# Routing to the experts: from phases of its own into the second attention stage

## The chip, the core and the metric

The program runs on one core of one Trainium2 chip (trn2). The metric is the device time of one execution in microseconds: the median of three runs. TensorE (PE) multiplies matrices and transposes, VectorE (DVE) and ScalarE (ACT) work element by element, GpSimd (POOL) works element by element and issues indirect DMAs, SyncE (SP) issues all other DMAs. Each engine runs its own instructions in the order in which they are written; between engines only semaphores order them.

## The reference

Two layers. Each adds a cross attention of `x` (32 x 112 x 256) over a context (32 x 375 x 256, 16 heads of 16), gated by a tanh, and then a gated feed-forward part. The first layer's is three matrices of plus and minus one (256, 1024, 1024, 256) with ReLU between. The second layer's is a mixture of 8 experts: each of the 3584 rows goes to the expert with the largest logit, and each expert takes the first 448 rows that choose it:

```python
    probs = jax.nn.softmax(xf.astype(jnp.float32) @ Wr, axis=-1)
    eidx = jnp.argmax(probs, axis=-1)
    p_tok = jnp.take_along_axis(probs, eidx[:, None], axis=1)[:, 0]
    onehot = jax.nn.one_hot(eidx, E, dtype=jnp.int32)
    rank_all = jnp.cumsum(onehot, axis=0) - onehot
    rank = jnp.take_along_axis(rank_all, eidx[:, None], axis=1)[:, 0]
    keep = rank < cap
    ...
    xe = xf[dispatch]
    h = jnp.maximum(jnp.einsum('ecd,edf->ecf', xe, W1), 0.0)
    ye = jnp.einsum('ecf,efd->ecd', h, W2)
```

`xf` is the layer-normalised output of the second attention; `ye`, times the row's probability and a gate, is added to the row it came from. The rank of a row among those of its expert depends on all rows before it.

## The kernel before

The program is a sequence of phases, each a block in which every engine has its own list of instructions; at the end of a phase all engines meet and SP clears the phase's semaphores one by one (L93 to L97): setup, queries 0, attention 0, FFN, queries 1, attention 1, then `moe_phases`: logits, ranks, experts.

**Attention** (`attention_phase`, used for both layers) is unrolled over 32 batch rows. In step `s` five rows are in work at once, `p`, `g`, `x`, `d`, `e` being the rows 1 to 5 steps back: `p`'s keys are made (`make_keys`, with a low half `k_low` from VectorE, L1053, on which the second half of the keys and the values wait), `x`'s values are made and its row maxima reduced (`rows`, 16 of them, through a ring of three PSUM banks), `d`'s scores go in 12 units through TensorE (`score_unit`), ScalarE's exponential (`weigh_up`, L947) and POOL's mask (`mask_unit`, L697; POOL masks 8 of the 12), and are multiplied with the values at the end of the step (`weigh`); `e`'s heads are turned, normalised, turned back, projected (L851) and added to `x_sum` (`add_output`, L1046), which SP stores. The order within a step is written out by hand in each engine's `body`. The head bank (bank 6) and the work bank (bank 7) each serve several of these in turn.

**The FFN** takes groups of four batch rows, eight groups. A group goes through 16 tiles `z`: 8 of the first inner layer (4 matmuls each) and 8 of the second (16 each), four PSUM banks in turn; each tile is split by ScalarE and VectorE (`low_hidden`, L1214) into a high and a low half. Between them the next group `s` is normalised: statistics behind tile 4 (`normalise`, L1185), scaling behind tile 6 (`normalise_end`, L1199), transposes behind tile 11 (`turn`), their low half behind tile 12, the mask's transposes behind tile 13. VectorE also makes the next attention's masks behind tiles 8 to 10 (L1227 to L1239).

**The logits phase** loads the second attention's output again in groups of four, normalises it, turns it (L1450) and multiplies it with the router's matrix in fp32 (L1441). **The ranks phase** finds for all 32 rows at once the largest logit, the probability, and the rank: one product with a triangle of ones counts within a batch row, one with all ones makes the rows' totals, and a scan of VectorE additions makes the running sums. **The experts phase** begins with 32 indirect DMAs of POOL, one per batch row, which write the normalised rows, their weight and their number to `expert_in` (L1706). SP issues the weights of expert 0, waits for all scatters, and loads the rows (L1671 to L1678). ScalarE and VectorE split the weights (L1765, L1805) and rows (L1790, L1830) into high and low halves; L1738 and L1752 are the experts' two layers, L1696 the gather of the old rows and L1701 the scatter of the results.

## Time and profile before

| | us |
|---|---|
| median of 3 runs (1806.5 to 1809.34) | 1806.68 |
| the profiled execution | 1801.03 |
| its span, first to last instruction | 1799.0 |
| TensorE busy | 1509.3 (84%) |
| VectorE, ScalarE, POOL busy | 1081.4, 800.7, 848.6 |

The span in 40 slices of 45 us, busy share in tenths:

```profile
PE   1739999999997799999957379999999995509996
DVE  4727777777774455555437267777777763515663
ACT  3316666666664222222213146666666652114441
POOL 1347777777775000000013447777777761064332
PEclk9959999999998899999988589999999996559999
```

Slices 4 to 13 are the first attention, 14 to 21 the FFN, 24 to 33 the second attention, 34 to 36 logits, ranks and scatter, the last four the experts. Times of instructions below are from this one profiled execution. A row of a timeline with `x8` stands for eight instructions in succession; the time is from the first's start to the last's end. Matmuls are pipelined: two starts 0.19 us apart, not the 0.35 us of each, say how long one holds the engine.

### The profile page before, as it was taken

The page shows a single profiled execution, that of the slowest core. Times are in us where ns is not written, and L with a number is a line of the kernel's source. Part 1 is how long each engine was busy: PE and PEld are TensorE (multiplying, and loading weights), DVE is VectorE, ACT ScalarE, POOL GpSimd, SP SyncE. Part 2 cuts the span into 40 slices and gives each one's busy share as a digit, 9 for nine tenths or more (in the row PEclk, how much of TensorE's full clock was granted, in tenths as well). Part 3 has the DMA queues.
Part 4 walks back from the last instruction along what each step waited for, and adds up shares of the span by engine and source line. Part 5 has one row for each costly group of instructions (what it writes and reads, how often), then busy time and mean ns, then how long its engine had stood idle before and what let it go on. Part 6 is the DMA issues. An engine that isn't in the chain of part 4 may idle for free. (4 is left out here: it accounts for less than half of the span.)

```text
span 1799.0 us, 40766 instructions
## 1 busy us (share of the span) xinstructions
PE 1509.3 (84%) x15271; PEld 1089.3 (61%) x15271; DVE 1081.4 (60%) x3493; ACT 800.7 (45%) x1822; POOL 848.6 (47%) x794
## 2 busy tenths in 40 slices
PE   1739999999997799999957379999999995509996
PEld 0317777777775356655633157777777774507775
DVE  4727777777774455555437267777777763515663
ACT  3316666666664222222213146666666652114441
POOL 1347777777775000000013447777777761064332
PEclk9959999999998899999988589999999996559999
DMA  7654454444430212222127545665565622035440
GB/s 230 220 105 96 95 111 105 97 104 107 100 80 20 59 59 64 69 91 60 33 76 224 95 106 122 126 117 116 113 128 116 110 45 69 26 120 171 134 149 17
DMA packets 225378, 183.62 MB, mean 102 GB/s; under 512 B 70314, under 2 KB 218735, under 8 KB 225192
## 3 DMA queue, kind: packets, MB, share of 16 engines
q1 hardware_dynamic: 219560, 171.36, 40.1%
q0 software_dynamic: 5632, 9.78, 1.7%
q8 instruction: 117, 1.92, 0.5%
q14 instruction: 69, 0.57, 0.1%
HBM read 99.53 MB, written 48.49 MB: 82 GB/s over the span
## 5 line engine op out<-in xcount | busy, mean ns | idle before, releaser
L947 ACT ACTIVATE probs_a<-bank 125x448 f32<-125x448 f32 x768 | 387.9, 541 | 27.4 <-PE bank L807 11.3
L697 POOL TENSOR_TENSOR probs_a<-probs_a,keep_a 125x448 int32<-125x448 int32 x256 | 285.0, 1135 | 122.1 <-ACT probs_a L947 121.9
L697 POOL TENSOR_TENSOR probs_a<-probs_a,mask_keep 125x448 int32<-125x448 int32 x256 | 285.1, 1135 | 105.6 <-ACT probs_a L947 105.4
L1021 DVE CUSTOM_DVE_ANT_0 masked_scores_a<-bank,mask_add_a 112x375 bf16<-112x375 f32 x512 | 259.4, 546 | 111.1 <-PE bank L778 107.2
L1021 DVE CUSTOM_DVE_ANT_0 masked_scores_a<-bank,mask_add 112x375 bf16<-112x375 f32 x512 | 259.3, 546 | 92.2 <-PE bank L778 88.6
L778 PE MATMUL bank<-k_stack_a,q_stack_a 96*128 96x375 f16 x1024 | 292.5, 327 | 9.6 <-issue 3.0
L807 PE MATMUL bank<-q_stack_a,k_stack_a 97*128 97x224 f16 x1536 | 252.4, 259 | 11.2 <-DMA q_stack_a<-max_t_a 10.3
L1335 PE MATMUL bank<-h0h_f,ffn_w 128*128 128x448 f16 x512 | 180.7, 353 | 10.8 <-DVE h0l_f L1214 10.8
L807 PEld LDWEIGHTS bank<-q_stack_a,k_stack_a 97*128 97x128 f16 x1536 | 145.8, 98 | 71.3 <-DMA q_stack_a<-max_t_a 11.8
L1335 PE MATMUL bank<-h0l_f,ffn_w 128*128 128x448 f16 x512 | 180.5, 353 | 0.0
L1174 POOL DMA_DIRECT2D x_after_ffn<-y_f x8 | 5.9, 741 | 344.7 <-DVE y_f L1221 344.7
L823 PE MATMUL bank<-probs_a,values_a 125*32 125x112 f32 x6144 | 161.7, 260 | 2.9 <-POOL probs_a L697 2.9
L823 PEld LDWEIGHTS bank<-probs_a,values_a 125*32 125x32 f32 x6144 | 144.8, 110 | 23.9 <-issue 19.6
L705 POOL TENSOR_TENSOR ctx_low_a<-ctx_in_a,ctx_high_a 128x375 f16<-128x375 f32 x128 | 112.9, 903 | 69.6 <-ACT ctx_high_a L925 69.6
L778 PEld LDWEIGHTS bank<-k_stack_a,q_stack_a 96*128 96x128 f16 x1024 | 99.6, 98 | 53.5 <-DVE row_max_a L1021 11.2
L747 PE MATMUL bank<-ctx_high_a,wk_high 128*128 128x375 f16 x256 | 87.2, 340 | 53.3 <-POOL ctx_low_a L705 48.5
L970 ACT ACTIVATE heads_t_a<-bank 128x448 f32<-128x448 f32 x64 | 34.8, 543 | 217.3 <-PE bank L823 217.3
L1286 ACT ACTIVATE h1h_f<-bank 128x448 f16<-128x448 f32 x64 | 34.8, 543 | 167.1 <-PE bank L1335 167.1
L1214 DVE SCALAR_TENSOR_TENSOR h1l_f<-bank,h1h_f 128x448 f16<-128x448 f32 x64 | 40.0, 624 | 111.1 <-ACT h1h_f L1286 111.1
L768 PE MATMUL bank<-wv_high,ctx_high_a 128*128 128x256 f16 x384 | 104.9, 273 | 1.6 <-DVE k_low_a L1053 1.5
L768 PE MATMUL bank<-wv_high,ctx_low_a 128*128 128x256 f16 x384 | 104.6, 272 | 0.0
L768 PE MATMUL bank<-wv_low,ctx_high_a 128*128 128x256 f16 x384 | 104.5, 272 | 0.0
(201 smaller groups left out, 3121.5 us busy)
## 6 DMA issues: line engine op xcount, KB each, us to landing
k_stack_a<-k_high_a SPq DMA_DIRECT2D x256, 96.0 KB, 4.1
ctx_in_a<-in_ctx_dram SPq DMA_DIRECT2D x64, 375.0 KB, 3.4
w_in_e<-in_L_ffn_W_dram SPq DMA_DIRECT2D x16, 1024.0 KB, 8.4
k_stack_a<-k_low_a SPq DMA_DIRECT2D x128, 96.0 KB, 4.3
q_stack_a<-q_split SPq DMA_DIRECT2D x128, 84.0 KB, 3.3
x_and_bias<-xb_q SPq DMA_DIRECT2D x16, 448.0 KB, 4.4
q_split<-high_q SPq DMA_DIRECT2D x32, 224.0 KB, 3.8
x_sum_a<-x_and_bias SPq DMA_DIRECT2D x64, 112.0 KB, 4.2
```

Source lines behind the costliest of these rows:

```text
L697: pool.tensor_tensor(bits, bits, cols, ALU.mult).then_inc(masked, 1)
L705: pool.tensor_tensor(ctx_low[s.four][:, cols], ctx_in[s.two][:, c, :], ctx_high[s.four][:, cols], ALU.subtract).then_inc(ctx_low_ready, 1)
L747: last = pe.matmul(work_bank[:, 0:S2], w[:, c, j * P:(j + 1) * P], part[p.four][:, c * S2:(c + 1) * S2], start=c == 0 and n == 0, stop=c = ...
L768: last = pe.matmul(work_bank[:, (k % 2) * D:(k % 2 + 1) * D], part[x.four][:, at:at + P], w[:, c, :], start=c == 0 and n == 0, stop=c == K ...
L778: pe.matmul(bank_of(x, h)[:, 0:S2], q_stack[x.four][0:STACK, at:at + P], k_stack[x.four][0:STACK, (h // 2) * WIDE:(h // 2) * WIDE + S2], s ...
L807: last = pe.matmul(bank[:, half * 2 * S:(half + 1) * 2 * S], k_stack[d.four][0:ROWS, at:at + P], q_stack[d.four][0:ROWS, (2 * t + half) * ...
L823: last = pe.matmul(head_bank[QUAD * j:QUAD * (j + 1), t * S:(t + 1) * S], values[d.two][:, k, 4 * t + j, :], probs[:, i, j * S:(j + 1) * S ...
L947: act.activation(probs[:, i, :], score_bank[i % 3][0:CK, 0:GT], ACT.Exp, scale=DK ** -0.5).then_inc(exped, 1)
L970: act.activation(heads_t[:, :], head_bank[:, 0:GT], ACT.Copy).then_inc(heads_ready, 1)
L1021: dve.tensor_tensor_reduce(masked_scores[:, use_of[x.value, h] % 3, :], bank_of(x, h)[0:S, 0:S2], mask_add[x.four][:, 0:S2], 1.0, -LARGEST ...
L1214: dve.scalar_tensor_tensor(out=low[:, j, :], in0=z_bank[z % 4][:, 0:GT], scalar=0.0, in1=high[:, j, :], op0=ALU.max, op1=ALU.subtract).the ...
L1335: last = pe.matmul(z_bank[z % 4][:, 0:GT], w[layer][:, c, j * P:(j + 1) * P], part[:, c, :], start=c == 0 and n == 0, stop=c == chunks - 1 ...
```

## The change

Three parts.

1. `logits_phase` and `ranks_phase` are gone, and the 32 scatters at the head of the experts phase with them. Their work is done inside attention 1, for row `f` (6 steps back) the normalisation and transposes, for `r` (7 back) the router's product, for each quad of four rows (`t`, 11 back) choice, count, order and place, and for `w` (15 back) the scatter. `run_quads` runs on for 15 steps beyond row 31 instead of 5; in the steps 37 to 46 only this work is left. The standard deviation's inverse is a power of -0.5 taken by POOL on one element per partition (`take_root`) between the third and the fourth mask of a step. The running sums over the batch rows are products: `before` (the triangle) times the row's choice, `ones` times the choices of the rows ahead in the quad and times `carried`, five small bf16 matmuls every fourth step. They, the router's product and the transposes use parts of the head bank, between `turn_heads_back` and the next `weigh`, and `weigh` waits until ScalarE has copied them out.
2. `x_sum` has four buffers instead of two, in both attentions; SP's reload of one waits for `xn_ready` too.
3. In the FFN the next group's statistics stand behind tile 9 and its scaling behind tile 11, the turn behind 12, the low half behind 13, the mask's transposes behind 14.

```diff
-        attention_phase(nc, m, 1, based, out, a["ctx_1024"], (add_1, keep_1), q_split)
-        moe_phases(nc, m, a, expert_in, out)
+        attention_phase(nc, m, 1, based, out, a["ctx_1024"], (add_1, keep_1), q_split, (a["L1_ffn_Wr"], expert_in))
+        experts_phase(nc, m, a, expert_in, out)
...
-        x_sum = many(2, sb, "x_sum", [S, D], F32)
+        x_sum = many(4, sb, "x_sum", [S, D], F32)
...
+            def take_root(f):
+                pool.wait_ge(measured, 4 * f.value + 3)
+                wait(pool, xn_ready, f.value)
+                pool.tensor_tensor(root[:, :], spread[:, :], half[:, :], ALU.pow).then_inc(rooted, 1)
...
+            def send_rows(w):
+                pool.wait_ge(routed, routed_at(w.quad, "put"))
+                pool.wait_ge(numbered, w.quad + 1)
...
+                pool.indirect_dma_start(expert_in[:, :],
+                                        bass.IndirectOffsetOnAxis(put[w.quad % 3][:, w.four:w.four + 1], 0),
+                                        sent_rows[:, at, :], None, bounds_check=E * CAP - 1,
+                                        oob_is_err=False).then_inc(sent[at], 16)
...
                 for i in pool_units:
+                    if i == pool_units[3] and layer and f.exists(B):
+                        take_root(f)
                     if d.exists(B):
                         mask_unit(d, i)
...
+                    t, w = s.back(13), s.back(15)
+                    if t.exists(B) and t.four == 0:
+                        number_tokens(t.quad)
+                    if w.exists(B):
+                        send_rows(w)
...
+            def route_products(s, e):
+                f, r, t = s.back(6), s.back(7), s.back(11)
+                counts = t.exists(B) and t.four == 1
...
+                pe.wait_ge(back_ready, min(e.value + 1, B))
+                wait(pe, routes_kept, routes(s.value) - 1)
+                if r.exists(B):
...
+                        last = pe.matmul(head_bank[0:S, 256:256 + E], xt[r.two][:, c, :], wr[:, c, :],
+                                         start=c == 0, stop=c == KC - 1)
+                if counts:
+                    pe.wait_ge(routed, routed_at(t.quad, "chosen"))
+                    dst = head_bank[0:S, 288:288 + G * E].rearrange("s (b e) -> s b e", b=G)
+                    pe.matmul(dst, before[:, :], chosen[:, :, :], start=True, stop=False, skip_group_check=True)
...
+                if f.exists(B):
+                    pe.wait_ge(xn_ready, f.value + 1)
+                    for c in range(KC):
+                        last = pe.transpose(head_bank[:, c * S:(c + 1) * S],
+                                            sent_rows[:, f.value % (3 * G), c * P:(c + 1) * P], ident[0:S, 0:S])
...
+                if layer:
+                    wait(pe, routes_kept, routes(d.value + 4))
...
+            def normalise_rows(f):
+                act.wait_ge(measured, 4 * (f.value + 1))
+                wait(act, sent[f.value % (3 * G)], 16 * (f.value // (3 * G)))
+                act.activation(sent_rows[:, f.value % (3 * G), 0:D], x_sum[f.four][:, :], ACT.Identity,
+                               bias=shift[:, 0:1], scale=root[:, 0:1]).then_inc(xn_ready, 1)
...
+            def measure(f, part):
+                if part == 0:
+                    dve.wait_ge(summed, f.value + 1)
+                    dve.bn_stats(stats[:, :], x_sum[f.four][:, :]).then_inc(measured, 1)
+                    return
...
+                if part == 3:
+                    dve.wait_ge(rooted, f.value + 1)
+                    wait(dve, xn_ready, f.value)
+                    dve.scalar_tensor_tensor(out=shift[:, :], in0=mean_var[:, 0:1], scalar=-1.0, in1=root[:, :],
+                                             op0=ALU.mult, op1=ALU.mult).then_inc(measured, 1)
...
                 rows(2, 3)
+                rows_measured(0)
                 if p.exists(B):
                     low_keys(p, 0)
-                rows(4, 5, 6, 7)
+                rows(4)
+                rows_measured(1)
+                rows(5)
+                rows_measured(2)
+                rows(6, 7)
+                rows_measured(3)
                 if p.exists(B):
                     low_keys(p, 1)
...
-            run_quads(B, 5, body)
+            run_quads(B, LAG, body)
...
-                        if z == 4:
+                        if z == 9:
                             normalise(s)
-                        if z == 6:
+                        if z == 11:
                             normalise_end(s)
-                        if z == 12:
+                        if z == 13:
                             low_rows(s)
```

TensorE, in a step of attention 1, from the row maxima's product 11 of row `x` (L778) over its values (L768) to product 12; before:

```order
L778 MATMUL bank<-k_stack_a,q_stack_a 128x375
...
L768 MATMUL bank<-wv_high,ctx_high_a 128x256
L768 MATMUL bank<-wv_low,ctx_high_a 128x256
L768 MATMUL bank<-wv_high,ctx_low_a 128x256
L768 MATMUL bank<-wv_high,ctx_high_a 128x256
...
L768 MATMUL bank<-wv_high,ctx_low_a 128x256
L778 MATMUL bank<-k_stack_a,q_stack_a 128x375
```

After, where L885 are the row maxima, L844 the values, L861 the router's product and L875 the transposes of the normalised rows:

```order
L885 MATMUL bank<-k_stack_a,q_stack_a 128x375
...
L844 MATMUL bank<-wv_high,ctx_high_a 128x256
L844 MATMUL bank<-wv_low,ctx_high_a 128x256
L844 MATMUL bank<-wv_high,ctx_low_a 128x256
L861 MATMUL bank<-wr_a,xt_a 112x8 x2
L875 MATMUL bank<-ident,sent_rows_a 128x112 x2
L844 MATMUL bank<-wv_high,ctx_high_a 128x256
L844 MATMUL bank<-wv_low,ctx_high_a 128x256
L844 MATMUL bank<-wv_high,ctx_low_a 128x256
...
L844 MATMUL bank<-wv_high,ctx_low_a 128x256
L885 MATMUL bank<-k_stack_a,q_stack_a 128x375
```

The router's product (two fp32 matmuls here, each two passes in a trace) and two transposes stand between the values' first and second part; every fourth step five more products stand between those two.

VectorE, in the same step, from row maxima 3 to 5 and on to the heads' normalisation (L1021 are the maxima, L1053 the low halves of the keys, L1036 and L1040 the heads); before:

```order
L1021 ISA masked_scores_a,row_max_a<-bank,mask_add_a 112x375
L1021 ISA row_max_a 112x1
L1053 SCALAR_TENSOR_TENSOR k_low_a<-bank,k_high_a 128x375
L1021 ISA masked_scores_a,row_max_a<-bank,mask_add_a 112x375
...
L1053 SCALAR_TENSOR_TENSOR k_low_a<-bank,k_high_a 128x375
L1036 RECIPROCAL inverse_a<-bank 112x16
L1040 TENSOR_TENSOR heads_q_a<-bank,inverse_a 112x256
```

After, where L1266 are the maxima, L1298 the low halves of the keys and L1281 the heads:

```order
L1266 ISA masked_scores_a,row_max_a<-bank,mask_add_a 112x375
...
L1176 BN_STATS stats_a<-x_sum_a 112x6
L1298 SCALAR_TENSOR_TENSOR k_low_a<-bank,k_high_a 128x375
...
L1180 BN_AGGR mean_var_a<-stats_a 112x2
L1266 ISA masked_scores_a,row_max_a<-bank,mask_add_a 112x375
...
L1184 TENSOR_SCALAR spread_a<-mean_var_a 112x1
L1266 ISA masked_scores_a,row_max_a<-bank,mask_add_a 112x375
...
L1188 SCALAR_TENSOR_TENSOR shift_a<-mean_var_a,root_a 112x1
L1298 SCALAR_TENSOR_TENSOR k_low_a<-bank,k_high_a 128x375
L1281 RECIPROCAL inverse_a<-bank 112x16
L1285 TENSOR_TENSOR heads_q_a<-bank,inverse_a 112x256
```

The statistics stand ahead of the first low half, the aggregate and the sum with epsilon behind the maxima 4 and 5, and `shift`, which waits for POOL's root, ahead of the second low half.

VectorE in the FFN, from the first inner layer's tile 4 (`h0l`) on (`stats`, `scale`, `xn` belong to the next group); before:

```order
L1214 SCALAR_TENSOR_TENSOR h0l_f<-bank,h0h_f 128x448
...
L1185 BN_STATS stats_f<-xg_f 112x6 x4
...
L1189 BN_AGGR mean_var_f<-stats_f 112x2 x4
...
L1214 SCALAR_TENSOR_TENSOR h0l_f<-bank,h0h_f 128x448
L1194 RECIPROCAL scale_f<-dev_f 112x4
...
L1199 TENSOR_SCALAR xn_f<-xg_f,mean_var_f,scale_f 112x256 x4
...
L1214 SCALAR_TENSOR_TENSOR h0l_f<-bank,h0h_f 128x448
```

After, from the second inner layer's tile 9 (`h1l`) on:

```order
L1481 SCALAR_TENSOR_TENSOR h1l_f<-bank,h1h_f 128x448
...
L1498 TENSOR_REDUCE seen<-mask_f_f 112x4
...
L1500 TENSOR_SCALAR cut_f<-seen 112x4
L1452 BN_STATS stats_f<-xg_f 112x6 x4
...
L1456 BN_AGGR mean_var_f<-stats_f 112x2 x4
...
L1481 SCALAR_TENSOR_TENSOR h1l_f<-bank,h1h_f 128x448
```

The statistics have moved from between `h0l` splits to behind the mask's reduction (`seen`, `cut`), ahead of the split of tile 10.

## Rows read from the trace of the kernel before

**Rows 1.** windows, seam and steady second attention: busy (instructions), clock, DMA, GB/s

```profile
1498.65:1620.53 121.88, 41.84 (x204) 37.72 (x205) 45.84 (x157) 19.18 (x37) 33.83 (x46) 0.50 0.26 81
1069.90:1481.40 411.50, 404.63 (x5382) 315.88 (x5384) 300.87 (x1148) 263.19 (x638) 309.74 (x291) 1.00 0.57 111
```

**Rows 2.** timeline across the seam: start, us, instruction, [idle before <- releaser]

```profile
1498.23 0.42 DVE L1046 TENSOR_TENSOR x_sum_a<-bank,x_sum_a 112x256 f32<-112x256 f32 x1 [3.23 <-PE bank L851]
...
1504.28 0.40 SPq L1419 DMA_DIRECT2D wr_l<-in_L_ffn_Wr_dram  x1
...
1570.63 0.20 DVE L1609 COPY rows_r<-token_k 112x32 int32<-112x32 int32 x1
...
1571.83 0.38 SPq L1671 DMA_DIRECT2D w_in_e<-in_L_ffn_W_dram  x1
...
1572.70 1.03 POOL L1706 DMA_INDIRECT expert_in<-rows_r,put_r  x1 [12.93 <-issue]
...
1611.70 0.94 POOL L1706 DMA_INDIRECT expert_in<-rows_r,put_r  x1 [0.30 <-issue]
...
1613.90 0.33 SPq L1678 DMA_DIRECT2D xg_e<-expert_in  x1
...
1620.53 0.53 PE L1738 MATMUL bank<-x_high_e,w_high_e 128*128 128x448 f16 x1 [1.38 <-DVE x_low_e L1830]
```

**Rows 3.** timeline, expert 0's splits of weights and rows

```profile
1581.18 4.27 ACT L1765 ACTIVATE w_high_e<-w_in_e 128x512 f16<-128x512 f32 x8 [21.17 <-DMA w_in_e<-in_L_ffn_W_dram]
...
1581.84 4.99 DVE L1805 SCALAR_TENSOR_TENSOR w_low_e<-w_in_e,w_high_e 128x512 f16<-128x512 f32 x8 [7.74 <-ACT w_high_e L1765]
...
1619.02 1.37 DVE L1830 TENSOR_TENSOR x_low_e<-bank,x_high_e 128x448 f16<-128x448 f32 x2 [32.19 <-ACT x_high_e L1790]
```

**Rows 4.** waits, 1050 to 1480: us in total, times, longest

```profile
PE bank L807 <- DMA q_stack_a<-max_t_a: 10.3, 9, 4.5
```

**Rows 5.** TensorE's timeline: one attention step, and the router's product

```profile
1276.02 0.32 PE L747 MATMUL bank<-ctx_high_a,wk_high 128*128 128x375 f16 x1
...
1278.66 0.28 PE L768 MATMUL bank<-wv_high,ctx_high_a 128*128 128x256 f16 x1
...
1279.87 0.36 PE L838 MATMUL bank<-ident,heads_q_a 112*128 112x112 f32 x2
...
1280.06 0.36 PE L807 MATMUL bank<-q_stack_a,k_stack_a 97*128 97x224 f16 x2
...
1553.66 3.15 PE L1441 MATMUL bank<-wr_l,xt_l 128*112 128x8 f32 x16 [0.63 <-ACT xt_l L1468]
```

**Rows 6.** VectorE's timeline: low halves of the keys, the router's statistics

```profile
1275.25 0.55 DVE L1053 SCALAR_TENSOR_TENSOR k_low_a<-bank,k_high_a 128x375 f16<-128x375 f32 x1
...
1277.81 0.55 DVE L1053 SCALAR_TENSOR_TENSOR k_low_a<-bank,k_high_a 128x375 f16<-128x375 f32 x1
...
1508.87 1.41 DVE L1489 BATCH_NORM_STATS2 stats_l<-xg_l 112x6 f32<-112x256 f32 x4 [10.21 <-DMA xg_l<-out_dram]
```

**Rows 7.** POOL's timeline: low contexts and masks of a step, and the iota

```profile
1270.41 1.76 POOL L705 TENSOR_TENSOR ctx_low_a<-ctx_in_a,ctx_high_a 128x375 f16<-128x375 f32 x2
...
1275.66 3.32 POOL L697 TENSOR_TENSOR probs_a<-probs_a,keep_a 125x448 int32<-125x448 int32 x3 [0.19 <-ACT probs_a L947]
...
1559.49 0.28 POOL L1541 IOTA token_k<- 112x32 int32 x1
```

**Rows 8.** TensorE's timeline in the FFN, end of the first inner layer

```profile
689.38 0.35 PE L1335 MATMUL bank<-h0l_f,ffn_w 128*128 128x448 f16 x1
...
691.22 0.36 PE L1335 MATMUL bank<-h0h_f,ffn_w 128*128 128x448 f16 x1 [1.48 <-DVE h0l_f L1214]
```

**Rows 9.** groups by line, FFN (560 to 920): busy us, mean ns, idle before

```profile
L1231 DVE TENSOR_REDUCE seen<-mask_f_f 112x4 f32<-112x1500 f32 (+1 forms) x8 | 13.6, 1704 | 0.0
L1185 DVE BATCH_NORM_STATS2 stats_f<-xg_f 112x6 f32<-112x256 f32 x32 | 11.2, 411 | 9.9 <-DMA xg_f<-x_after_attention 9.9
L1199 DVE TENSOR_SCALAR xn_f<-xg_f,mean_var_f,scale_f 112x256 f32<-112x256 f32 x32 | 11.1, 409 | 0.7
```

439 lines of the change are left out of this document (207 added, 232 removed).

## The prediction

> **What bounds the kernel now.** I first cut the span into stretches (the table of windows), then read the timeline around the seam that the change takes away, and last the steady part of the second attention stage, since that is where the work goes.
>
> The seam: between the last addition of the second attention (VectorE, ends 1498.65) and the first matmul of expert 0 (1620.53) lie 121.88 us, a third of them with TensorE busy, at a granted clock of 0.50, so the 1.2 GHz level [rows 1]. In order of time [rows 2]: the stage ends and its semaphores are cleared, first DMA of the logits phase at 1504.28; logits and ranks until 1570.83; first weight DMA of the experts at 1571.83; 32 scatters on POOL from 1572.70 to 1611.70, so (1611.70 - 1572.70) / 31 = 1.26 us each; the load of their rows issued at 1613.90; first matmul at 1620.53. Expert 0's weights are ready long before and hidden by the scatter: ScalarE splits them from 1581.18, VectorE until 1581.84 + 4.99 = 1586.83 [rows 3].
>
> The second attention: TensorE is busy 404.6 of 411.5 us at full clock (2.4 GHz) [rows 1], and its only long wait there is 10.3 us, in the first steps [rows 4]. Thirty steps fill that stretch, 13.7 us each, and in a step its instructions stand end to end. Here every instruction added to TensorE lengthens the step, while ScalarE (263 of 411), VectorE (301) and POOL (310) have room on average.
>
> **Term 1, the seam.** T is the end of the last addition. New, behind T:
> - VectorE chain for the last batch row, its four instructions and the hop to POOL and back: statistics 0.4 (1.41 for four, 0.35 apart), then small ones at 0.20 each, as the last of the ranks phase [rows 2, 6], the root on POOL, together 1.4.
> - ScalarE's row 0.4, two transposes 0.6 at the low clock, copy 0.4, four half-clock passes of the router 4 x 0.197 (3.15 / 16 [rows 5]) = 0.8 plus 0.2 of pipeline, copy 0.2: 2.6, so T + 4.0.
> - Five VectorE operations 1.0, five small products 0.9, copy 0.3, then six VectorE operations 1.3 with hops: `put` of the last quad at T + 7.7.
> - POOL meanwhile has ten scatters left: it is in step 37 when T comes, because `take_root` of row 31 stands ahead of them. Six of them (rows 22 to 27) run 7.5 us from T + 1.2 to T + 8.7, the `iota` to T + 9.0, so it is POOL and not the VectorE chain that is late; four more end at T + 14.0. Landing takes 1613.90 - 1611.70 = 2.2 [rows 2]: T + 16.2.
> - End of stage: 1504.28 - 1498.65 - 2.2 (store landing like the scatter) = 3.4 with 44 semaphores cleared; 1571.83 - 1570.83 = 1.0 with 5; so 0.06 each, and 70 cost 3.4 + 1.6 = 5.0. First weight DMA at T + 21.2.
> - The cover of the weight load is gone: from issue to the last split is 1586.83 - 1571.83 = 15.0, and `x_low` (1.37, behind it on VectorE [rows 3]) makes 16.4. First matmul at T + 37.6.
> Saved: 121.9 - 37.6 = 84.3 us. What is late now is the weight load, no longer the scatter. Bounds: if the ten scatters were all done at T, 8 us more; if each takes a quarter longer beside other work, 4 less.
>
> **Term 2, the steps of the second attention.** TensorE gets per step, in front of the second part of the values: two fp32 transposes, as L838's, which hold it 1280.06 - 1279.87 = 0.19 [rows 5]; the router's two fp32 products, four passes, at 1.2 GHz 0.197 each, at 2.4 GHz half of it, 0.4; every fourth step five small bf16 products at about 0.1, as a transpose, 0.5 / 4 = 0.12. Sum 0.7. Their inputs are there: `xn` is made by ScalarE some 1 us earlier, `back_ready` before the first values.
>
> VectorE gets 0.35 for the statistics ahead of the first `k_low` and three small operations before the second. The first `k_low` ends at 1275.80 and TensorE's next keys begin at 1276.02; the second ends at 1278.36 and the values begin at 1278.66 [rows 5, 6]. So slack is 0.22 and 0.30. The statistics use it up, 0.35 - 0.2 = 0.15; the small ones, issued between pipelined operations, shift the second by 0.1 each, of which the slack and the delay that TensorE already has take most: 0.1 is left. The four route operations behind row 8 use the idle time before row 12, nothing on the path. Stall 0.25.
>
> The unknown is `pow` on POOL: no row shows it. VectorE needs its result after row 7, about 1278.2, POOL can begin it when it has finished three masks, 1275.66 + 3.32 less the third, so 1277.9 [rows 7]. Nearest rows: an `iota` of 112x32, 0.28; a mask of 125x448, 1.1. One element per partition is nearer to the first: I take 0.3, no stall beyond the above; at 1.1 it would cost 0.8 a step more. Below nothing it cannot be, it replaces nothing. POOL's own load: 8 masks of 3.32 / 3, low contexts 1.8, scatter 1.26, `pow` 0.3, `iota` 0.1, so 12.3 of 13.7 [rows 1, 2, 7]; the scatter stands behind `ctx_low`, where POOL idles now until the next step's exponentials. ScalarE gets 0.4 + 0.2 + 0.35, mostly where it waits for the values.
>
> 28 full steps carry this (6 to 33): 28 x 0.95 = 26.6, and the three draining steps 34 to 36 at half clock about 0.5 each. Cost 28 us; by TensorE's terms alone 20, with `pow` as a mask 50.
>
> **Term 3, the FFN.** In the first inner layer a tile is four matmuls 0.19 apart, 0.76 us, and VectorE's split of it takes nearly as long. The normalisation of the next group pushed in between, (11.2 + 11.1) / 8 = 2.8 us with some 0.5 of small ones [rows 9], drains the four banks: from 689.38 to 691.22 TensorE stands where 0.19 is usual, 1.65 us too long [rows 8], in each of seven groups. In the second layer a tile takes 16 x 0.19 = 3.0. New there: tile 9 carries its split, the mask's reduction of 13.6 / 8 = 1.7, and 1.4 of statistics [rows 9], with the small ones 4.4 us, which is 1.4 over, and tile 10 has 1.1 spare; `xn` is then ready about 3.0 us after tile 11 is, just when TensorE has done tile 12 and wants it. I price that at 0 to 0.3 a group. Saved 7 x 1.65 = 11.6, and some tenths from the smaller hesitation ahead of it, less 0.7: 11.5. Bounds 6 and 13.
>
> **Small ones.** Eleven memsets more at the second stage's start, four more semaphores in the first: 1 us. The four buffers for `x_sum` change no wait that shows.
>
> **Sum.** 84.3 + 11.5 - 28 - 1 = 66.8 saved of the span 1799.0, so 1732.2. The profiled execution took 1801.03, 2.0 more than its span, and the median of three is 1806.68, 5.65 above that execution. 1732.2 + 2.0 + 5.7 = 1739.9; I say 1740.
>
> **Rules of the skill.** Five microseconds of the 32 scatters ran beside VectorE's weight splits [rows 2, 3], and the mean distance is 1.26 all the same; no row has them in an attention step. By the Trainium skill ("SBUF — State Buffer", the section on SBUF's two separate sides) POOL cannot write descriptors while VectorE runs an operation in a two-port mode, and such a DMA took 3.1 us instead of 0.62. That is the mechanism of the second rival, whose price comes from rows.
>
> The `iota` of the ranks phase, the first of the whole program, took 0.28 us [rows 7]. The Trainium skill ("GPSIMD Engine Reference", Instruction dispatch) has the first call of freshly loaded code pay about 6 us. Paid once it changes nothing here; paid each time POOL goes from one function to another it would be the last rival.
>
> **Rivals.**
> 1. VectorE's chain over POOL becomes the step's bound: `pow` costs 1 us or more, and the second `k_low`, the values and all behind them wait for it. For: slack before the values is 0.30 us only. Against: a tiny operand. At 1.4 us, 1.1 x 28 = 31 more: 1771. Chance 0.16.
> 2. POOL is full: scatters slowed by VectorE's work from 1.26 to 3 us make its step 12.3 + 1.7 = 14.0 beside waits that it can't skip, 0.5 to 1 us a step, and 10 x 1.7 in the tail: some 35 more, 1775. Against: the scatter stands where POOL idles most of its 13.7 - 309.7 / 30 = 3.4 us [rows 1]. Chance 0.06.
> 3. The stage swallows it: TensorE's instructions hide behind the weigh phase, cost 5 to 10 instead of 28: 1720. For: VectorE and ScalarE wait there for TensorE; against: TensorE itself does not wait [rows 1, 4]. Chance 0.12.
> 4. Slower than before: POOL's change between mask, `pow`, `iota` and scatter costs microseconds each time. It decides from 66.8 / 28 = 2.4 us a step beyond mine, so from a `pow` of 2.7 us; at 6 us the time is 1740 + 28 x 5.7 = 1900. Nothing in the rows speaks for it. Chance 0.03.
> 5. Only the FFN part does not do what it says (the new place stalls as long as the old): 1752, inside my own range. That the experts would not start earlier can't be: nothing but the phases removed stood before them.
>
> **Numbers.** My case 0.63, its own range 1726 to 1756. With rivals 1 and 3 taken in: 1718 to 1772, leaving out most of 2 and 4. A difference under 0.2% (3.6 us) could not be told from none; faster 0.96, same 0.01, slower 0.03.
>
> **What would show it.** Right: about 38 us from the last addition to the first expert matmul, with expert 0's split, not a scatter, in front of it; an attention step of 14.6 to 14.8; an FFN group of 38.8 instead of 40.55; POOL's last four scatters back to back. Wrong: VectorE waiting for POOL's root in every step, a step over 15.5, or scatters well over 1.3 us apart.

## The result, and the profile after

The changed kernel takes 1840.47 us (median of 4 runs, 1838.85 to 1842.33) beside 1806.59 for the kernel before on the same chip: a ratio of 1.0184, 95% interval 1.0169 to 1.0200. It is slower by 34 us where 1740 was forecast. The span of its profiled execution is 1838.0 us, 39.0 more than before. The forecast had three terms, and the two traces show each of them:

| stretch of the span, us | before | after | difference | forecast |
|---|---|---|---|---|
| start to first addition of attention 1 (VectorE, `x_sum`) | 1075.28 | 1063.62 | -11.7 | -11.5 and +1 |
| first to last addition, 31 steps | 422.95 | 560.49 | +137.5 | +28 |
| end of the last addition to the first expert matmul | 121.88 | 38.02 | -83.9 | -84.3 |
| from there to the end | 178.47 | 175.45 | -3.0 | 0 |

Two terms came out as worked. The span was forecast 66.8 us shorter and is 39.0 longer, a miss of 106; the steps of the second attention alone are 110 over, and the other rows take 4 off again. The 3.0 us of the last row were not looked into. The windows of after, stretch and length in us, then busy time and instruction count of TensorE, its weight loads, VectorE, ScalarE and POOL, then granted clock, DMA share, GB/s; the first row answers to the first of [rows 1], the other two to the second:

```profile
1624.53:1662.55 38.02, 4.01 (x20) 3.11 (x21) 12.29 (x38) 6.75 (x16) 13.98 (x16) 0.50 0.44 140
...
1085.00:1217.00 132.00, 122.62 (x1552) 93.46 (x1551) 101.23 (x383) 86.97 (x216) 95.61 (x96) 1.00 0.54 110
1230.00:1570.00 340.00, 283.31 (x3224) 209.32 (x3221) 237.92 (x795) 174.32 (x431) 206.74 (x209) 0.90 0.44 84
```

TensorE, busy 404.6 of 411.5 us before, now stands for 9 us of 132, and later for 57 us of 340, at a granted clock of 0.90. The steps show two regimes: the additions are 15.65 us apart from 1080 to 1221, where the first scatter comes (1223.40), then mostly 20.0 (16.3 to 21.9). Before they were 13.73 apart in a full step without a wait.

The seam, answering to [rows 2] and [rows 3]: the last of POOL's scatters, which come 1.25 us apart there, the first weight DMA, expert 0's splits, the first expert matmul.

```profile
1637.65 0.94 POOL L753 DMA_INDIRECT expert_in<-sent_rows_a,put_a  x1 [0.30 <-issue]
1647.65 0.40 SPq L1692 DMA_DIRECT2D w_in_e<-in_L_ffn_W_dram  x1
...
1655.77 4.27 ACT L1777 ACTIVATE w_high_e<-w_in_e 128x512 f16<-128x512 f32 x8 [24.38 <-DMA w_in_e<-in_L_ffn_W_dram]
1656.43 4.90 DVE L1817 SCALAR_TENSOR_TENSOR w_low_e<-w_in_e,w_high_e 128x512 f16<-128x512 f32 x8 [6.51 <-ACT w_high_e L1777]
...
1661.26 1.14 DVE L1842 TENSOR_TENSOR x_low_e<-bank,x_high_e 128x448 f16<-128x448 f32 x2
...
1662.55 0.53 PE L1750 MATMUL bank<-x_high_e,w_high_e 128*128 128x448 f16 x1 [3.36 <-DVE x_low_e L1842]
```

The waits of after from 1050 to 1580 (us in total, times, longest), where [rows 4] had only one wait of TensorE, for a DMA:

```profile
PEld bank L844 <- DVE k_low_a L1298: 69.3, 27, 4.1
PE bank L844 <- DVE k_low_a L1298: 62.6, 27, 3.8
...
DVE shift_a L1188 <- POOL root_a L739: 14.1, 28, 1.2
```

TensorE waits for `k_low` 27 times, 2.3 us each. `k_low` itself still takes 0.54 us. The reader should now ask what stands ahead of it on VectorE. First POOL, then VectorE, in a step of 20 us (answering to [rows 6] and [rows 7]):

```profile
1405.93 0.57 POOL L739 TENSOR_TENSOR root_a<-spread_a,half_a 112x1 f32<-112x1 f32 x1
1406.48 3.29 POOL L734 TENSOR_TENSOR probs_a<-probs_a,keep_a 125x448 int32<-125x448 int32 x3
```

```profile
1404.95 0.15 DVE L1184 TENSOR_SCALAR spread_a<-mean_var_a 112x1 f32<-112x1 f32 x1
...
1406.53 3.26 DVE L1188 SCALAR_TENSOR_TENSOR shift_a<-mean_var_a,root_a 112x1 f32<-112x1 f32 x1 [0.51 <-POOL root_a L739]
1409.71 0.54 DVE L1298 SCALAR_TENSOR_TENSOR k_low_a<-bank,k_high_a 128x375 f16<-128x375 f32 x1
```

`shift`, one element in each of 112 partitions, takes 3.26 us: it begins 0.05 us behind the start of POOL's next masks and ends with the last of the three (1409.79 and 1409.77). `spread`, as small but with one tensor input, took 0.15 us beside a mask. In the first ten steps `shift` took 1.08 us, what one mask takes:

```profile
1119.58 3.33 POOL L734 TENSOR_TENSOR probs_a<-probs_a,keep_a 125x448 int32<-125x448 int32 x3
```

```profile
1119.64 1.08 DVE L1188 SCALAR_TENSOR_TENSOR shift_a<-mean_var_a,root_a 112x1 f32<-112x1 f32 x1 [0.33 <-POOL root_a L739]
```

Length goes with spacing. Wherever the three masks behind the root take 3.31 to 3.33 us, `shift` takes 1.08 or 1.09 and gets in behind the first; wherever they take 3.29, it is held over all three; at 3.30 both occur. The likely reading is a hair's breadth between two masks in which VectorE gets its turn, but no row shows the gap itself. It is not `shift` that makes it: in the kernel before, masks in a row take 3.32 as well [rows 7]. Where POOL is idle, in the tail, `shift` takes 0.16 us. The Trainium skill ("SBUF — State Buffer", section "Who interferes with whom") says just this: of two inputs in SBUF, VectorE reads the second through a port pair that it shares with GpSimd, whoever is first holds it for its whole instruction, and the other stands. By that rule, the trace agrees; the rule does not say that the wait can span several instructions of POOL, and here it spans three.

The stall costs a second time. TensorE, which had stood for 3.39 us, goes on at full clock (granted 1.00 from 1410.3 to 1411.3), is at the 1.2 GHz level from 1411.6 to 1415.0 (granted 0.50), though it does not stand there, and is then back at full clock; starts of the values are 0.11, 0.21 and again 0.11 us apart:

```profile
1410.31 0.28 PE L844 MATMUL bank<-wv_high,ctx_high_a 128*128 128x256 f16 x1 [3.39 <-DVE k_low_a L1298]
1410.43 0.27 PE L844 MATMUL bank<-wv_low,ctx_high_a 128*128 128x256 f16 x1
...
1412.51 0.42 PE L844 MATMUL bank<-wv_high,ctx_high_a 128*128 128x256 f16 x1
1412.73 0.42 PE L844 MATMUL bank<-wv_low,ctx_high_a 128*128 128x256 f16 x1
...
1415.03 0.27 PE L844 MATMUL bank<-wv_low,ctx_high_a 128*128 128x256 f16 x1
1415.14 0.27 PE L844 MATMUL bank<-wv_high,ctx_low_a 128*128 128x256 f16 x1
```

From the first addition to the end of the last TensorE stands for 560.91 - 479.35 = 81.6 us, 423.37 - 412.22 = 11.2 before: 70 of the 137.5 us are stalls, 67 longer busy time. The kernel `quiet` below runs the same 5717 matmuls in this stretch at a granted clock of 1.00 and is busy 439.02 us, so only 27 of the 67 are new work, and about 40, an estimate from these, are the lower clock (0.92 over the stretch).

### The profile page after: what moved, and what is told of

It is laid out like the page before. It is cut to its first block and busy times, and to the rows that moved or that the text cites. A ratio compares the mean times of both kernels' runs of the same rounds, so it can differ in the third digit from the quotient of the medians.

```text
span 1838.0 us, 41279 instructions
## 1 busy us (share of the span) xinstructions
PE 1539.9 (84%) x15307; PEld 1095.0 (60%) x15307; DVE 1140.2 (62%) x3609; ACT 827.2 (45%) x1907; POOL 864.4 (47%) x824
## 5 line engine op out<-in xcount | busy, mean ns | idle before, releaser
L1266 DVE CUSTOM_DVE_ANT_0 masked_scores_a<-bank,mask_add_a 112x375 bf16<-112x375 f32 x512 | 265.3, 543 | 145.1 <-PE bank L885 144.4
L1266 DVE CUSTOM_DVE_ANT_0 masked_scores_a<-bank,mask_add 112x375 bf16<-112x375 f32 x512 | 259.3, 546 | 92.0 <-PE bank L885 88.4
L885 PE MATMUL bank<-k_stack_a,q_stack_a 96*128 96x375 f16 x1024 | 298.8, 333 | 9.5 <-DVE row_max_a L1266 3.3
L914 PE MATMUL bank<-q_stack_a,k_stack_a 97*128 97x224 f16 x1536 | 260.7, 265 | 6.7 <-DMA q_stack_a<-max_t_a 5.7
L914 PEld LDWEIGHTS bank<-q_stack_a,k_stack_a 97*128 97x128 f16 x1536 | 150.0, 100 | 69.2 <-DMA q_stack_a<-max_t_a 6.0
L844 PE MATMUL bank<-wv_high,ctx_high_a 128*128 128x256 f16 x384 | 112.4, 293 | 64.1 <-DVE k_low_a L1298 64.0
L885 PEld LDWEIGHTS bank<-k_stack_a,q_stack_a 96*128 96x128 f16 x1024 | 101.2, 99 | 57.3 <-DVE row_max_a L1266 11.8
L844 PE MATMUL bank<-wv_low,ctx_high_a 128*128 128x256 f16 x384 | 111.6, 291 | 0.0
L844 PE MATMUL bank<-wv_high,ctx_low_a 128*128 128x256 f16 x384 | 111.5, 290 | 0.0
```

Of the source, the lines that this page charges most:

```text
L844: last = pe.matmul(work_bank[:, (k % 2) * D:(k % 2 + 1) * D], part[x.four][:, at:at + P], w[:, c, :], start=c == 0 and n == 0, stop=c == K ...
L885: pe.matmul(bank_of(x, h)[:, 0:S2], q_stack[x.four][0:STACK, at:at + P], k_stack[x.four][0:STACK, (h // 2) * WIDE:(h // 2) * WIDE + S2], s ...
L914: last = pe.matmul(bank[:, half * 2 * S:(half + 1) * 2 * S], k_stack[d.four][0:ROWS, at:at + P], q_stack[d.four][0:ROWS, (2 * t + half) * ...
L1266: dve.tensor_tensor_reduce(masked_scores[:, use_of[x.value, h] % 3, :], bank_of(x, h)[0:S, 0:S2], mask_add[x.four][:, 0:S2], 1.0, -LARGEST ...
```

## Experiments

Theory A: VectorE's instructions with two inputs in SBUF are held by POOL's masks. Theory B: the way over POOL for the root is what costs. Theory C, which came up on the way: A, and VectorE's instructions with one input are held too when they have several elements per partition. Ratios are to the kernel before on the same chip, with their 95% interval; where two kernels are compared in us, it is by their ratios, times 1804.

**one_input**: the changed kernel, `shift` with one tensor input.

```diff
-                    dve.scalar_tensor_tensor(out=shift[:, :], in0=mean_var[:, 0:1], scalar=-1.0, in1=root[:, :],
-                                             op0=ALU.mult, op1=ALU.mult).then_inc(measured, 1)
+                    dve.tensor_scalar(shift[:, :], mean_var[:, 0:1], root[:, 0:1], -1.0, ALU.mult,
+                                      ALU.mult).then_inc(measured, 1)
```

> The changed kernel, with shift computed by an instruction that has one tensor input (mean) and takes root as a scalar per partition; nothing else differs. Theory A (an instruction of VectorE with two SBUF tensor inputs stands until POOL's masks that run back to back are over): shift takes about 0.15 us as spread's tensor_scalar does in the same steps, never 1.08 or 3.26; the second k_low is late only by the wait for root (0.33 to 0.5 us); steps of 15.0 us instead of 15.65 and 20, so the stage from first to last addition is about 465 us instead of 560 and the time 1840 - 95 = 1745 us. Theory B (what costs is the wait for POOL's pow and the way there and back, and the recorded length of shift is only how that wait is written down): shift stays at 1 to 3 us in whatever form, 1840 us.

Measured: 1784.65 us, ratio 0.9898 (0.9880 to 0.9915). `shift` takes 0.21 us in all 32 steps, so B's claim about its length falls. But by the ratios only 52 of the 95 us came back: steps are 15.17 us and from the first scatter on 16.8. What is left stands next to `shift` in the trace: `max_parts`, which took 0.16 us in the changed kernel, takes 0.98 once a step and from the first scatter on mostly 2.07 or 2.08.

```profile
1240.40 0.21 DVE L1188 TENSOR_SCALAR shift_a<-mean_var_a,root_a 112x1 f32<-112x1 f32 x1 [0.68 <-POOL root_a L739]
1241.61 2.08 DVE L1275 TENSOR_SCALAR max_parts_a<-row_max_a 112x8 f16<-112x8 f32 x1
```

**late_one**: the same, and `shift` behind the second `k_low`.

```diff
-                rows_measured(3)
                 if p.exists(B):
                     low_keys(p, 1)
+                rows_measured(3)
```

> As one_input, and shift stands behind the second k_low instead of ahead of it. Theory A with the root's wait as a second, smaller cost: VectorE's wait for root no longer holds up k_low, steps of 14.6 us, 5 to 12 us less than one_input, so about 1735 us. If the wait for root costs nothing once shift is short: same as one_input.

Measured: 1779.03 us, 0.9873 (0.9851 to 0.9895), 44 us over the 1735 expected, and not clear of one_input (the intervals overlap). The first ten steps are 14.60 to 15.04 us, where 14.6 was forecast for all; then 15.3 to 15.8, and 18.7 to 20.3 in every fourth. In those the second victim, an instruction that the change had not touched, is held longest:

```profile
1219.96 3.63 DVE L1275 TENSOR_SCALAR max_parts_a<-row_max_a 112x8 f16<-112x8 f32 x1
```

**late_two**: the move alone, `shift` with two inputs.

> The changed kernel, shift with its two tensor inputs kept, but behind the second k_low. Theory A: shift still takes 1 to 3.3 us beside POOL's masks, but TensorE's values no longer wait for k_low; late instead are heads_q and the row maxima behind shift, for which TensorE has some 0.6 us of room: of 3.26 us about 2.6 stay, of 1.08 about 0.4. Between 1780 and 1830 us. Theory B (only k_low's wait for the root costs): near 1740 us, as moving it takes the wait off the path.

Measured: 1793.88 us, 0.9947 (0.9924 to 0.9970), in A's range. `shift` takes 1.05 or 3.26 us behind `k_low` too.

**maxima**: `late_one`, with `max_parts` made by a reduction.

```diff
                 act.activation(max_t[half][:, :], bank_of(n, HALVES[half])[:, :].bitcast(F16)[0:HH, 0:S],
-                               ACT.Copy).then_inc(max_ready, 1)
+                               ACT.Copy, scale=-1.0).then_inc(max_ready, 1)
...
-                dve.tensor_scalar(max_parts[:, half, 0:HH], row_max[:, cols], -1.0, None, ALU.mult).then_inc(parts_ready, 1)
+                dve.tensor_reduce(max_parts[:, half, 0:HH], row_max[:, cols].unsqueeze(2), AX.X,
+                                  ALU.max).then_inc(parts_ready, 1)
```

> As late_one, and the instruction that makes max_parts, one input, 112x8, which took up to 3.63 us beside masks in late_one, becomes a reduction over an axis of one, with the sign moved to ScalarE's copy of the turned maxima. Theory C (VectorE's instructions that POOL's masks hold are those with two SBUF inputs and those with one and more than one element; statistics and reductions, 0.17 to 0.2 us everywhere, are not): max_parts 0.2 us, steps of 14.6 us, and 15 to 17 only where choice, count, order and place stand (four instructions each, 0.5 us too long): 1735 us. If max_parts is held in this form too: 1779 us as late_one.

Measured: 1735.71 us, 0.9625 (0.9593 to 0.9656): as expected, and 45 us better than late_one by changing the form of one instruction. Steps are 14.60 us, 14.86 to 15.05 where the route's instructions stand between the rows. There most of those with two SBUF inputs, and the `tensor_scalar`s with one input and several elements, take 0.7 to 0.86 us; the reductions take 0.17, and so does the reciprocal of 112x4 with one SBUF input, so C holds for `tensor_scalar` and not for every form. Groups of VectorE from 1100 to 1450 (busy us, mean ns):

```profile
L1216 DVE TENSOR_TENSOR chosen_a<-number_a,first_a 112x32 bf16<-112x32 f32 x5 | 4.3, 859 | 0.0
L1205 DVE SCALAR_TENSOR_TENSOR marked_a<-shifted_a,number_a 112x32 f32<-112x32 f32 x6 | 4.2, 705 | 0.0
L1248 DVE TENSOR_SCALAR over_a<-rank_a 112x4 f32<-112x4 f32 x5 | 4.2, 834 | 0.0
...
L1209 DVE TENSOR_REDUCE first_a<-marked_a 112x4 f32<-112x32 f32 x6 | 1.0, 174 | 0.0
```

**quiet**: `maxima`, with choice, count, order and place at the end of the step before; ScalarE's part of them, `power_up`, comes a step earlier too.

```diff
-                rows(8)
-                route(t, 0)
...
-                rows(12)
+                rows(8, 9, 10, 11, 12)
...
                 if x.exists(B):
                     shift_parts(x, 1)
+                for part in range(4):
+                    route(s.back(10), part)
```

> As maxima, and the instructions for choice, count, order and place stand at the end of the step before, behind row 15, where VectorE waits 2 us for TensorE and POOL is idle, instead of behind rows 8 to 11. All of theory C: no instruction of VectorE is held for longer than 0.3 us, every full step takes 14.6 to 14.8 us, which is what the prediction priced: 1730 us. If steps stay over 15 us, something else than VectorE's held instructions lengthens them.

Measured: 1726.45 us, 0.9584 (0.9555 to 0.9612), the fastest: it beats the kernel before by 4.2% and the changed one by 5.9%. Most steps are 14.60 us, before the first scatter and after; from its first to its last addition it takes 445.95 us. Its window from 1070 to 1450 has TensorE busy 378.87 of 380 us at full clock:

```profile
1070.00:1450.00 380.00, 378.87 (x4892) 288.73 (x4891) 285.85 (x1194) 257.46 (x655) 305.46 (x306) 1.00 0.58 114
```

Now single parts put back onto `quiet`.

**quiet_early**: `shift`, one input, ahead of `k_low` again.

> quiet with shift in its form with one tensor input, but ahead of the second k_low. What is left is VectorE's wait for POOL's root: 0.33 us and shift's own 0.2. Steps of 15.15 us as in the first ten of one_input instead of 14.60: 28 x 0.55 = 15 us more than quiet, 1741 us.

Measured: 1741.27 us, 0.9669 (0.9646 to 0.9693), 15 us more than quiet, as expected. The steps are 14.78, later 15.30 us. The wait for the root, with the 0.2 us of `shift` itself, is all there is to theory B.

**quiet_two**: `shift` in the form and place of the changed kernel.

> quiet with shift as in the changed kernel: two SBUF inputs, ahead of the second k_low; max_parts and the route's instructions stay as in quiet. Held for one mask each time (1.08 us), steps of 15.65 us as in the first ten of the changed kernel: 28 x 1.05 = 29 us more than quiet, 1756 us. Held for all three (3.26 us) as in the changed kernel from the first scatter on: steps of about 20, another 90 us, 1840 us. If neither (under 10 us more), shift was not what cost and max_parts or the route's instructions were.

Measured: 1803.54 us, 0.9989 (0.9961 to 1.0018), 73 us more than quiet: between the two. Up to the first scatter `shift` takes 1.08 us and steps are 15.65; from then on it takes 1.09 in most steps (16.2 to 16.4 us long) and 3.26 in every fourth (22.7 to 22.9).

**quiet_eight**: `max_parts` in its old form.

> quiet with max_parts in its old form (one input, 112x8). In late_one it began 0.3 us ahead of the end of a mask and took 0.26 us in three steps of four, and 2.5 to 3.6 us in the fourth, where the masks ran without any gap; those steps took 18.7 to 20.3 us. If the route's instructions between the rows were what closed the gap, nothing is held now and the time is quiet's, 1727 us. If the scatters close it: 7 steps with 4 us more, 1755 us.

Measured: 1771.45 us, 0.9822 (0.9799 to 0.9845), 43 us more than quiet, more than either guess. It takes 3.62 us in six steps, all behind the first scatter and the last of them draining (0.35 at most in the other full steps), so it is not the route's instructions that close the gap. POOL's masks in such a step end at 1258.47, and it at 1258.50:

```profile
1254.08 4.39 POOL L734 TENSOR_TENSOR probs_a<-probs_a,keep_a 125x448 int32<-125x448 int32 x4
```

```profile
1254.88 3.62 DVE L1276 TENSOR_SCALAR max_parts_a<-row_max_a 112x8 f16<-112x8 f32 x1
```

**no_scatter**: the changed kernel without its `indirect_dma_start` and the waits for it; the experts then work on empty slots.

> The changed kernel without the 32 scatters (the experts then work on empty slots; all else is as it was). In the changed kernel's trace a step takes 15.65 us and shift 1.08 us until the step of the first scatter, and 20 us with 3.26 us of shift in most steps from then on. Theory S (the scatter, about 1.25 us on POOL, is what brings the masks end to end, so that shift waits for three instead of one): steps stay at 15.65 us, about 20 steps x 4.4 = 85 us less than the changed kernel, and some 10 us less in the tail: 1745 us. Rival (the instructions for choice, count, order and place, which begin at the same time, are what does it): the steps of 20 us stay, 1830 us.

Measured: 1760.23 us, 0.9750 (0.9723 to 0.9776). All full steps stay at 15.65 us (15.9 in some) and `shift` at 1.08, so theory S holds: in the full steps the second regime comes with the scatters. A scatter is not the only way to it, though: in the last three steps that still have masks `shift` takes 3.25 here too, with three masks in 3.29 or 3.30. It is 78 us from the changed kernel; I had worked out 95.

The other side of the matter is the kernel before itself, with one instruction added per step of the second attention. Its own trace already has the effect. In two draining steps, where POOL's eight masks run in a row, `max_parts` is seven times as long as in a full step:

```profile
1461.17 1.13 DVE L1030 TENSOR_SCALAR max_parts_a<-row_max_a 112x8 f16<-112x8 f32 x1
...
1473.95 1.14 DVE L1030 TENSOR_SCALAR max_parts_a<-row_max_a 112x8 f16<-112x8 f32 x1
```

**lone_two**, **lone_one**, **lone_eight**: on VectorE, behind row 7, with two inputs, with one, and with one and eight elements per partition. The edit of lone_two, without the tiles and their memsets:

```diff
                 rows(4, 5, 6, 7)
+                if layer and p.exists(B):
+                    dve.wait_ge(lone, p.value + 1)
+                    dve.scalar_tensor_tensor(out=lone_out[:, :], in0=lone_in[:, 0:1], scalar=-1.0, in1=lone_by[:, :],
+                                             op0=ALU.mult, op1=ALU.mult).then_inc(lone, 1)
```

> The kernel before, and in each step of the second attention one more instruction on VectorE, between row 7 and the second k_low: 112 partitions, one element each, two SBUF tensors in, result used by nothing. Theory A (such an instruction stands until POOL's running mask, or the run of masks, is over): POOL's three masks run there until about 1279.0 in the step of rows 7, VectorE reaches the place at 1277.7, so it takes 0.2 to 1.3 us in most steps where an unhindered one takes 0.15; the second k_low and the values come that much later: 15 to 40 us more than before. Theory B (in the changed kernel it was the way over POOL that cost): this kernel has no such way, under 4 us more.

> As lone_two, but the added instruction has one tensor input and takes the other as a scalar per partition. Theory A: 0.15 to 0.21 us each, which the 0.3 us ahead of the values mostly hide: 0 to 4 us more than before. If any instruction added there costs what lone_two costs, the two are alike.

> As lone_two, but the added instruction has one SBUF tensor in and out with eight elements in each of 112 partitions, as max_parts has, which took 0.16 us where no mask ran and up to 3.63 us beside masks. Theory C (one tensor input is enough to be held when there is more than one element per partition): as lone_two, 15 to 40 us more. Theory A alone (two tensor inputs are needed): as lone_one, 0 to 4 us more.

Measured: 1.0000 (0.9986 to 1.0014), 0.9996 (0.9977 to 1.0015), 1.0008 (0.9989 to 1.0027). My expectation for the first and, by theory C, for the third failed, and I had read it off a sum of durations and not off the masks' own grid: in lone_two the instruction begins 0.06 us ahead of the end of a mask in nearly every step, and takes 0.15 us; in two steps, where it begins 0.13 us behind one's start, it takes 0.98, and lone_eight has two such of 1.01 and 0.99. These two thus told nothing apart in time.

**row5_two**: the same behind row 5.

> As lone_two (the kernel before with one added instruction of 112x1 with two SBUF inputs in each step of the second attention), but behind row 5 instead of row 7, 0.94 us earlier. In lone_two it began 0.06 us ahead of the end of a mask in nearly every step and took 0.15 us, and 0.98 us in the two steps where it began 0.13 us behind the start of one. Behind row 5 it begins some 0.1 us behind the start of a mask in every step: theory A gives 1.0 us or more each time, the second k_low 0.7 us late, and max_parts, which has a gap of 0.31 us between two runs of masks, then falls into the second run and is held as well: 20 us more than before at least, up to the 119 of lone_pow. If such an instruction is not held in this kernel: under 4 us more.

Measured: 0.9994 (0.9979 to 1.0009). Missed once more: the masks' grid moved along, and it now begins 0.12 us ahead of a mask's end.

**row4_two**: behind row 4.

> As row5_two, but behind row 4, 0.47 us earlier. In row5_two the added instruction began 0.12 us ahead of a mask's end (0.16 us), in the others 0.91 us (1242.11, 0.91 us behind its start of the second mask 0.23) and 1.04 us: it lasts until the running mask ends. So here about 0.6 us in nearly every step. That moves the rows behind it by 0.4; if the second k_low and max_parts move as far, max_parts misses its gap of 0.31 us: then 20 to 119 us more than before; if the wait for row 7 (0.14 us) and the slack take it up: under 10 us.

Measured: 1.0017 (1.0003 to 1.0031), 3 us more. POOL, then VectorE:

```profile
1278.91 3.33 POOL L699 TENSOR_TENSOR probs_a<-probs_a,keep_a 125x448 int32<-125x448 int32 x3 [0.43 <-ACT probs_a L949]
```

```profile
1279.43 0.63 DVE L1074 SCALAR_TENSOR_TENSOR lone_out_a<-lone_in_a,lone_by_a 112x1 f32<-112x1 f32 x1
```

The first mask ends at 1278.91 + 3.33 / 3 = 1280.02, the held instruction at 1280.06. It takes 0.63 us in 27 steps. What a held instruction takes is the rest of the mask that runs, and of those that follow it without a gap; the rows of the kernels above agree with it. A step is 0.21 us longer, and `max_parts` still finds its gap.

**lone_pow**: on POOL, the power alone, used by nothing.

```diff
                 for i in pool_units:
+                    if i == pool_units[3] and layer and d.exists(B):
+                        pool.wait_ge(lone, d.value + 1)
+                        pool.tensor_tensor(lone_out[:, :], lone_in[:, 0:1], lone_by[:, :], ALU.pow).then_inc(lone, 1)
                     if d.exists(B):
                         mask_unit(d, i)
```

> The kernel before, and on POOL one pow of 112x1 between the third and the fourth mask of each step of the second attention; VectorE is left as it was and nothing uses the result. The kernel before runs max_parts (one input, 112x8) for 0.16 us in nearly every step, just behind the last of POOL's three masks: 1279.11, with masks until 1278.98. Theory C: 0.56 us on POOL put the masks on top of max_parts, which then takes 0.7 to 3.3 us and delays the rows behind it: 10 to 60 us more. If POOL's time has room, as the prediction took it (3.4 us idle a step): under 3 us more.

Measured: 1927.81 us, 1.0657 (1.0623 to 1.0691): 119 us for an instruction of 0.55 us that nothing waits for, more than I had dared to expect. POOL, then VectorE:

```profile
1293.51 0.55 POOL L715 TENSOR_TENSOR lone_out_a<-lone_in_a,lone_by_a 112x1 f32<-112x1 f32 x1
1294.03 4.40 POOL L699 TENSOR_TENSOR probs_a<-probs_a,keep_a 125x448 int32<-125x448 int32 x4
```

```profile
1294.77 3.68 DVE L1037 TENSOR_SCALAR max_parts_a<-row_max_a 112x8 f16<-112x8 f32 x1
```

In the kernel before, POOL's masks of [rows 7] end at 1278.98 and the next three begin at 1279.29; `max_parts` runs in the 0.31 us between. The power fills that gap.

```profile
1279.11 0.16 DVE L1030 TENSOR_SCALAR max_parts_a<-row_max_a 112x8 f16<-112x8 f32 x1
```

```profile
1279.29 3.33 POOL L697 TENSOR_TENSOR probs_a<-probs_a,keep_a 125x448 int32<-125x448 int32 x3 [0.31 <-ACT probs_a L947]
```

**pow_reduce**: `lone_pow` with `max_parts` as in `maxima`.

> lone_pow with max_parts as a reduction over an axis of one and the sign moved to ScalarE's copy, as in maxima. If max_parts was all of the loss, max_parts takes 0.16 us, steps are back at 13.7 to 13.9 us and the time is within 5 us of the kernel before. If the masks coming 0.55 us later delay TensorE by themselves (it waits for them in the weighing): 10 us or more over the kernel before.

Measured: 1807.94 us, 1.0001 (0.9985 to 1.0018). All 119 us are gone and the power stays: its own time on POOL and the masks coming later cost under 4 us together, by the interval.

**ffn_only**: the kernel before with the FFN part alone.

> The kernel before with the FFN part of the change alone. From the trace of the changed kernel an FFN group takes 38.7 us instead of 40.2, and the first addition of the second attention comes 11.7 us earlier: so 11 to 12 us less than before, 1795 us (0.9935 of it). If the FFN part gives its gain back later (another wait in the queries phase behind it): under 6 us less.

Measured: 1788.78 us, 0.9924 (0.9906 to 0.9942), by the ratio 13.7 us less, in keeping with 11.7 in the trace of after. No later stage takes it back.

## Why the prediction was wrong

**Term 1, the seam**, right: 38.0 us for 37.6, with expert 0's splits and not a scatter in front, last scatters 1.25 us apart. The ten scatters behind T end at T + 14.1 for 14.0. That the sum fits to half a microsecond is partly luck, for two parts were off against each other: the first weight DMA comes at T + 23.1 for 21.2, since the end of the stage takes 1.9 us more than priced, and the weight load and splits take 14.9 for 16.4.

**Term 3, the FFN**, right: stores of the groups are (911.1 - 640.3) / 7 = 38.7 us apart, 38.8 forecast; alone it is worth 13.7 us where 11.5 was said.

**Term 2, the steps**, is where it failed. Not in the prices of the new work: in `quiet`, which has all of it, a step is 14.60 us for 13.73, 0.87 where I had 0.95, and the stage 23 us longer where I had 28; the whole kernel takes 1726 us, by its ratio 1731 beside the 1806.59 of the kernel before, inside the range of the forecast's own case. The power took 0.56 us for the 0.3 I took, and that by itself costs nothing. The step that failed is the sentence on VectorE's small instructions, "issued between pipelined operations, shift the second by 0.1 each". It priced `shift` at 0.1 us by its size. It takes 1.08 to 3.26 us, by what POOL does beside it, and the shift of 0.1 became a wait of TensorE for the second `k_low` of 2.3 us a step. Nor had the sum a term for the clock that falls behind such a stall, some 40 us of the stage. POOL's root was written out to be followed by three masks, and `shift` waits for the root, so it arrives just behind the start of a mask, the worst point there is.

I had the rule in hand. The prediction cited the shared port for one direction only, VectorE holding up POOL's scatters, as the mechanism of rival 2 at 0.06; that never showed (scatters take 0.98 to 1.06 us in the steps; in the tail 0.94 to 0.99, 1.25 us apart), and its price of 3 us a scatter, said to come from rows, stands in no row. The direction that mattered, POOL's masks holding up VectorE, stands in the same section of the Trainium skill's page, and [rows 7] with the masks in it lay in front of me: POOL was masking in 8 x 1.11 = 8.9 of 13.7 us. The `max_parts` of 1.13 us in the draining steps of the same trace went unread.

**Rival 1** (the chain over POOL becomes the bound) named the right place, the second `k_low` and the values behind it, and the wrong cause. What it meant, the wait for the root, is 15 us (quiet_early against quiet), where it had priced 31. Two of the signs named for being wrong came, a step over 15.5 us and VectorE waiting for the root in every step (0.33 to 0.5 us in most), and the second of them pointed at the smaller cost. **Rival 4**, the only one on the slower side, had POOL's change of function at microseconds each; POOL's next mask begins 0.55 us behind the start of the root. A rival with the cause found here was missing, so 0.03 stood on slower where much more was due.

How the 108 us between `quiet` (0.9584) and the changed kernel (1.0184) divide: the wait for the root 15 us, `shift`'s two inputs 58 more (quiet_two against quiet_early), the route's instructions between the rows 7 (maxima against quiet), with overlapping intervals. That leaves 28 for their acting together, which no kernel took apart. `max_parts`, 43 alone, is not in this sum: in the changed kernel `shift`'s stall pushes it behind the masks, where it takes 0.16 us (in one step 1.20); with `shift` repaired it comes back among them, which is why one_input gave back only half.

Open: why a scatter at the end of a step closes the gaps between masks. no_scatter shows that it does in the full steps (3.31 to 3.34 us for three masks against mostly 3.29); which wait of POOL vanishes was not tried. The runs show which forms are held and until when; that a shared port is what holds them is taken from the rule cited above, and no run looks at a port.

## What to carry to other kernels

Where GpSimd runs elementwise work from SBUF, as the masks here, an instruction of VectorE with two SBUF inputs, or a `tensor_scalar` with one and several elements per partition, costs what is left of GpSimd's instruction at that moment, and of those behind it where they leave no gap, whatever its own size. Read GpSimd's timeline at its place before pricing it, and give it one input and one element, or make it a reduction. Its recorded length shows it (1.08, 3.26, 3.62 us where 0.16 is usual), and so does the engine that waits behind it. A kernel can live off a gap of 0.3 us without anyone having written it down: compare the starts of what stands in it before adding anything to the other engine.

## What the runs showed of the hardware

- POOL's `pow` of 112x1 takes 0.54 to 0.58 us; a held instruction is not recorded as waiting but as busy.
- VectorE's instruction can be held over several of POOL's in succession when these run without a gap: over three masks in 3.29 us (after), over four in 4.39 and once over the power and four masks, 4.90 us (lone_pow). Three masks in 3.31 us or more let `shift` in behind the first.
- Not held beside masks: statistics (0.42 us), reductions (0.15 to 0.20), the reciprocal of 112x4 (0.16), the row maxima, the keys' low halves and the heads' products, each with one input from a PSUM bank and one from SBUF (0.54, 0.54 and 0.42), and one element per partition with one tensor input (0.14 to 0.22).
